# First stage of cross attention: rows of ones from another buffer, context in longer pieces, keys' weights in two parts, five values' jobs moved ahead

## The chip, the cores and the metric

The kernel runs as one program on one core of one Trainium2 chip. The metric is device time in microseconds (us) of one execution. The core has five engines that work side by side, each on its own list of instructions: PE (TensorE, matrix products), DVE (VectorE), ACT (ScalarE), POOL (GpSimd) and SP (SyncE, which here only issues DMAs). ACT issues DMAs as well. The 16 DMA engines serve both: what SP issues goes through queue q1, what ACT issues through queue q10. An engine waits for another, or for a DMA, by a semaphore (`wait_ge`).

## The reference, cut to what matters

One layer of a Perceiver: cross attention of 4 x 256 tokens on a context of 4 x 4096 rows, then attention in a window, then a mixture of 16 experts. Only the start of the first part is touched by the change.

```python
q = x @ wq.T + bq                       # x: layer norm of 4 x 256 x 256
k = y @ wk.T + bk                       # y: context, 4 x 4096 x 192
v = y @ wv.T + bv                       # 16 heads of 16
score = jnp.einsum('bhqd,bhkd->bhqk', q, k) * scale
attn = jax.nn.softmax(score, axis=-1)
out = jnp.einsum('bhqk,bhkd->bhqd', attn, v)
return out @ wo.T + bo
```

## The kernel before, in words

**Groups and steps.** Cross attention goes over 16 groups (4 batches x 4 groups of 4 heads), each of 32 steps of 128 context rows; n counts the 512 steps. Each score needs the largest score of its row first. So `max_pair(m)` computes scores with the queries as rows (2 matmuls per m, into three PSUM banks in turn) and DVE takes the largest of each (`max_one`, L1083); this runs LEAD = 36 steps ahead of the step that uses it. From n = 0 on, `scores(n)` computes the scores again with the keys as rows, ACT takes the exponential (L897), and `weigh` multiplies with the values (L537). Before n = 0 there are 36 steps with a max pair and side jobs only.

**Keys.** A job ("k", f) multiplies 2048 context rows with the keys' weights for one group (L421). ACT adds the bias into `key_low` (L884, L904), POOL splits it into a high part `key_high` and a rest `key_low` (L1447 to L1457), and SP lays both by DMA into `keys` (L1594), whose three rows 32 to 34 (and 96 to 98) of every slot must hold 1.0, so that the matmul adds the negative maximum. POOL writes 1.0 into `key_low` at the start (L1501) and SP lays it out from there into `keys` (L1617, semaphore ld_kones). Before the loop the first job is done in two halves, `keys_of(0, 0)` and `keys_of(0, 1)`, and ACT may write the first keys into `key_low` only when both DMAs that read the ones from it have landed (`e.wait_ge(ld_kones, 32)` ahead of `first_keys(0)`).

**Queries.** The first two tiles of x are normalised by DVE, turned by PE (L448), copied by ACT (L873), multiplied with `wq` (L457), taken by ACT with the bias (L878), split by POOL (L1462, L1464) and laid out by six DMAs that ACT issues (`load_q`, L396). `max_pair(0)` waits for these, for the first keys and for the ones.

**Values.** A job ("v", b, j) multiplies two tiles of context with the values' weights (L438, 6 matmuls in the program, 12 in the trace, since a float32 matmul is shown as two) and ACT empties the two PSUM banks (L910).

**The order.** It is written out by hand. `side_jobs(n)` says which side jobs stand at step n, `S_JOBS` is the list of all that use the PSUM banks S_BANKS in turn, and a job may start when ACT has emptied the one two places ahead (`bank_pair`). For batch 0 the values' jobs stand at every second step from n = -31. `turn_rows` (L466) and `q_rest` (L475) prepare the other queries.

**DMA queues.** SP issues in this order: first part of x, identf, wq, bq, rest of x, the ones (2 DMAs), the first keys, then wv, lsel, wo, bv, bo. ACT issues wk, bk and four pieces of the context (`ctx_in`).

Of the kernel before, what the change touches and what calls it, by code (L numbers as in the profile page):

```python
# [7 lines left out]
F32 = mybir.dt.float32  # L8
# [45 lines left out]
EARLY_FROM = 12  # L54
S_BANKS = (0, 2)
# [15 lines left out]
def side_jobs(n):  # L71
# [10 lines left out]
    if b < BATCH and off == 0 and 0 <= j < KT // 2:  # L82
        jobs.append(("v", b, j))
# [15 lines left out]
S_JOBS = [("k", 0)]  # L99
# [68 lines left out]
def build(nc, a, out, scratch):  # L168
    ctx = ExitStack()
    with ctx:  # L170
# [8 lines left out]
        def bank(i, n=1):  # L179
# [21 lines left out]
        ctx_in = s1.tile("ctx_in", (CB, KV // 2))  # L201
# [10 lines left out]
        wk = s1.tile("wk", (CB, EMB))  # L212
# [117 lines left out]
        ld_tok0, ld_tok1, ld_const, ld_wk, ld_wq, ld_w, ld_b, ld_c, ld_kones = semaphores(  # L330
            "ld_tok0", "ld_tok1", "ld_const", "ld_wk", "ld_wq", "ld_w", "ld_b", "ld_c", "ld_kones")
# [71 lines left out]
        def _(e):  # L403
# [5 lines left out]
            def keys_of(f, part=None):  # L409

                g, c = f // 2, f % 2 * 4
                if part is None:
                    bank_pair(("k", f))
                pairs = range(2) if part is None else (part,)
                for i in pairs:
                    e.wait_ge(ld_ctx[c // 2 + i], 16 * (g // NG + 1))
                for r in range(CB):
                    for i in pairs:
                        for odd in range(2):
                            rows, at = slice(64 * odd, 64 * odd + 64), (c // 2 + i) * CH  # L420
                            t = e.matmul(bank(S_BANKS[S_NO["k", f] % 2] + odd)[64 * i:64 * i + 64],  # L421
                                         wk[rows, r, g % NG * 64:g % NG * 64 + 64], ctx_in[rows, r, at:at + CH],
# [3 lines left out]
            def values_of(b, j):  # L426

                bank_pair(("v", b, j))
                if b == 0 and j == 0:
                    e.wait_ge(ld_w, 16 * 5)  # L430
# [3 lines left out]
                at = p * CH + j % (CH // P) * P  # L434
                for r in range(CB):
                    for odd in range(2):
                        rows = slice(64 * odd, 64 * odd + 64)
                        m = e.matmul(bank(first + odd)[:, 0:EMB], ctx_in[rows, r, at:at + P], wv[rows, r],  # L438
# [40 lines left out]
            def max_pair(m):  # L479
# [11 lines left out]
                if m == 0:  # L491
                    e.wait_ge(act_q, KE)
                    e.wait_ge(ld_kones, 32)
# [157 lines left out]
            first_queries(1)  # L651
            done_early = 0
# [217 lines left out]
        def _(e):  # L870
# [95 lines left out]
            first_queries(1)  # L966
            for n in range(-LEAD, STEPS):
# [473 lines left out]
        def _(e):  # L1441
# [59 lines left out]
            e.memset(key_low.bitcast(F32), 1.0).then_inc(pool_ones1, 1)  # L1501
# [15 lines left out]
            for n in range(-LEAD, STEPS):  # L1517
                for job in side_jobs(n):
                    if job[0] == "k":
                        split_keys(job[1])  # L1520
                    elif job == ("q", KE - 1):
# [3 lines left out]
                        e.wait_ge(ld_w, 16 * 5)  # L1525
# [59 lines left out]
        def _(e):  # L1585
# [18 lines left out]
            def load_ctx(b, p):  # L1604
                sl = slice(p * CH, (p + 1) * CH)
# [163 lines left out]
```

## Time and profile before

| | us |
|---|---|
| median of 3 runs | 1417.48 (1416.03 to 1417.87) |
| the profiled execution's own time | 1418.6 |
| its span (first to last instruction) | 1416.8 |
| PE busy | 1285.6 (91%) |
| DVE busy | 912.4 (64%) |
| ACT busy | 743.9 (53%) |
| POOL busy | 266.2 (19%) |

The whole span in 40 slices of 35.4 us, from the page (each digit is the busy share in tenths; PEld is PE loading weights, beside its matmuls):

```profile
PE   2689999999999999999999999997998729999996
PEld 1354444456444455544455544446777519999995
DVE  3478888676888767788866788627677552222224
ACT  0127777666777766677767677844555301111110
```

PE works in nine tenths and more of nearly every slice. The exceptions are the first three slices, the change from one part of the layer to the next, and the end. The change touches the first two or three slices. Times in the rows below are counted from the start of the span. A busy time is the sum of an engine's instructions; what an engine does while nobody waits for it costs nothing.

### The profile page before, as it was taken

What the parts mean: (1) busy time and instruction counts of PE and PEld (TensorE: products, weight loads), DVE (VectorE), ACT (ScalarE), POOL (GpSimd) and SP (SyncE); (2) the same over time, 40 slices, a digit from 0 to 9 for tenths busy, and PEclk for the clock granted to TensorE, in tenths of its full rate; (3) what the DMA queues carried; (4) which work ended last, traced back from release to release, by engine and by line L of the source; (5) the groups of instructions that cost most, each with busy time, mean ns of one, the idle gap of its engine ahead of it and who ended that gap; (6) DMA issues with size and microseconds to landing.
All of it is one profiled execution on the core that took longest, in us unless ns stands there. A gap on an engine that the chain in (4) does not pass through costs nothing.

```text
span 1416.8 us, 29928 instructions
## 1 busy us (share of the span) xinstructions
PE 1285.6 (91%) x12231; PEld 795.6 (56%) x12231; DVE 912.4 (64%) x1735; ACT 743.9 (53%) x1036; POOL 266.2 (19%) x245
## 2 busy tenths in 40 slices
PE   2689999999999999999999999997998729999996
PEld 1354444456444455544455544446777519999995
DVE  3478888676888767788866788627677552222224
ACT  0127777666777766677767677844555301111110
POOL 2231121211121111112112211101600012222210
PEclk7799999999999999999999999998999859999998
DMA  5735466344457334456533453100000039989852
GB/s 165 118 51 77 65 117 114 52 71 65 57 97 133 52 51 67 65 101 122 70 46 51 66 76 46 47 4 6 1 2 16 1 141 383 375 328 327 323 202 101
DMA packets 52426, 150.67 MB, mean 106 GB/s; under 512 B 17030, under 2 KB 21014, under 8 KB 44354
## 3 DMA queue, kind: packets, MB, share of 16 engines
q1 hardware_dynamic: 46562, 135.84, 43.5%
q0 software_dynamic: 2976, 8.13, 1.7%
q10 hardware_dynamic: 2752, 4.79, 1.1%
q8 instruction: 97, 1.59, 0.5%
q14 instruction: 39, 0.32, 0.1%
HBM read 88.63 MB, written 6.16 MB: 67 GB/s over the span
## 4 chain that ended last, share of the span: by engine, by line
PE 83%; DVE 7%; ACT 4%; DMA 2%; issue 2%; POOL 0%; ACTq 0%; SPq 0%; DVEq 0%; POOLq 0%
PE psum L537 19%; PE psum L519 14%; PE psum L497 10%; PE psum L829 8%; PE psum L841 8%; PE psum L438 7%; PE psum L421 6%; ACT wts L897 2%; PE psum L700 2%; DMA keys<-key_low 2%; DVE o_norm L1125 1%; PE psum L718 1%; PE psum L618 1%; DVE biased L1217 1%; DVE part_max L1083 1%
## 5 line engine op out<-in xcount | busy, mean ns | idle before, releaser
L1083 DVE TENSOR_REDUCE part_max<-psum 128x1 f32<-128x512 f32 x1024 | 656.2, 685 | 205.2 <-PE psum L497 203.8
L897 ACT ACTIVATE wts<-psum 128x1024 f32<-128x1024 f32 x512 | 515.5, 1023 | 92.1 <-PE psum L519 91.5
L537 PE MATMUL psum<-wts,vals 128*17 128x256 f32 x4096 | 317.3, 385 | 0.0
L519 PEld LDWEIGHTS psum<-queries,keys 51*128 51x128 f32 x2048 | 157.3, 185 | 201.0 <-issue 143.5
L519 PE MATMUL psum<-queries,keys 51*128 51x256 f32 x2048 | 260.2, 332 | 8.1 <-ACT wts L897 7.0
L497 PE MATMUL psum<-keys,queries 51*128 51x512 f32 x1024 | 229.4, 443 | 24.9 <-DVE part_max L1083 11.1
L1029 ACT ACTIVATE hid<-psum,b1s 128x128 f32<-128x128 f32 x124 | 35.4, 367 | 206.7 <-PE psum L829 170.0
L537 PEld LDWEIGHTS psum<-wts,vals 128*17 128x17 f32 x4096 | 69.5, 95 | 120.7 <-issue 97.2
L497 PEld LDWEIGHTS psum<-keys,queries 51*128 51x128 f32 x1024 | 97.2, 185 | 40.1 <-DVE part_max L1083 26.4
L829 PE MATMUL psum<-xTt,w1s 128*128 128x128 f32 x992 | 118.0, 278 | 0.0
L829 PEld LDWEIGHTS psum<-xTt,w1s 128*128 128x128 f32 x992 | 115.4, 195 | 0.3 <-issue 0.2
L841 PE MATMUL psum<-w2s,hid 128*128 128x256 f32 x496 | 112.0, 379 | 0.0
L1447 POOL CAST key_high<-key_low 128x1024 fp32r<-128x1024 f32 x31 | 32.1, 1037 | 407.0 <-ACT key_low L904 402.8
L421 PE MATMUL psum<-ctx_in,wk 64*64 64x512 f32 x768 | 97.8, 620 | 9.9 <-DMA ctx_in<-in_ctxT 9.9
L438 PE MATMUL psum<-wv,ctx_in 64*128 64x256 f32 x768 | 99.5, 392 | 0.0
L841 PEld LDWEIGHTS psum<-w2s,hid 128*128 128x128 f32 x496 | 91.9, 190 | 11.3
L1407 DVE TENSOR_SCALAR hid<-psum,b1s 128x128 f32<-128x128 f32 x124 | 34.9, 344 | 95.9 <-PE psum L829 95.9
L438 PEld LDWEIGHTS psum<-wv,ctx_in 64*128 64x128 f32 x768 | 70.9, 188 | 27.7 <-issue 16.4
L983 ACT ACTIVATE wt<-biased,nmax 128x160 f32<-128x160 f32 x128 | 44.3, 416 | 76.4 <-DVE nmax L1219 76.4
L910 ACT ACTIVATE vals<-psum 128x512 f32<-128x512 f32 x64 | 38.3, 598 | 86.2 <-PE psum L438 86.2
L904 ACT ACTIVATE key_low<-psum,bk 128x1024 f32<-128x1024 f32 x31 | 34.5, 1113 | 89.2 <-PE psum L421 89.2
L1449 POOL TENSOR_TENSOR key_low<-key_low,key_high 128x1024 fp32r<-128x1024 f32 x31 | 73.6, 2374 | 2.5
(180 smaller groups left out, 985.0 us busy)
## 6 DMA issues: line engine op xcount, KB each, us to landing
keys<-key_high SPq DMA_DIRECT2D x256, 128.0 KB, 4.5
w1s<-in_W SPq DMA_DIRECT2D x31, 1024.0 KB
w2s<-in_W SPq DMA_DIRECT2D x31, 1024.0 KB
keys<-key_low SPq DMA_DIRECT2D x128, 128.0 KB, 6.4
ctx_in<-in_ctxT SPq DMA_DIRECT2D x12, 768.0 KB, 9.2
ctx_in<-in_ctxT ACTq DMA_DIRECT2D x4, 768.0 KB, 22.4
queries<-query_high SPq DMA_DIRECT2D x60, 32.0 KB, 5.4
rows_x<-xn SPq DMA_DIRECT2D x2, 512.0 KB, 2.7
```

What stands on the lines that cost most here:

```text
L421: t = e.matmul(bank(S_BANKS[S_NO["k", f] % 2] + odd)[64 * i:64 * i + 64], wk[rows, r, g % NG * 64:g % NG * 64 + 64], ctx_in[rows, r, at:at ...
L438: m = e.matmul(bank(first + odd)[:, 0:EMB], ctx_in[rows, r, at:at + P], wv[rows, r], start=(r == 0), stop=(r == CB - 1))
L497: e.matmul(bank(M_BANKS[(2 * m + i) % 3]), queries[g % 3][64 * i:64 * i + STK, hh, qt * P:(qt + 1) * P], keys[64 * i:64 * i + STK, hh, slo ...
L519: m = e.matmul(bank(S_BANKS[S_NO["s", n] % 2] + i)[:, hh * SEQ:(hh + 1) * SEQ], keys[64 * i:64 * i + STK, hh, c, at:at + P], queries[g % 3 ...
L537: i = e.matmul(bank(O_BANK)[32 * j:32 * j + VW, 0:SEQ], vals[:, t, h * VW:(h + 1) * VW], wts[n % NW][:, j * SEQ:(j + 1) * SEQ], start=(t = ...
L829: i = e.matmul(bank(2 * (j % 2) + hb)[:, q * P:(q + 1) * P], w1s[j % RING][:, k, hc * P:(hc + 1) * P], xTt[j % 2][:, k], start=(k == 0), s ...
L841: i = e.matmul(bank(4 + j % 2)[:, 0:EMB], hid[j % 2][:, hc], w2s[j % RING][:, hc], start=(hc == 0), stop=(hc == HC - 1))
L897: i = e.activation(wts[n % NW], s_bank(job, 2), ACT.Exp, scale=QSCALE)
L910: i = e.activation(vals[:, t:last + 1:CH // P].rearrange("p t (h w) -> p t h w", w=VW)[:, :, :, 0:HD], s_bank(job, 2).rearrange("p (t h w) ...
L983: i = e.activation(wt2[r][:, j], biased[r][:, j], ACT.Exp, bias=nmax[r][:, j:j + 1])
L1083: e.reduce_max(part_max[g % 2][:, hq, c:c + 1], bank(M_BANKS[n % 3]), AX_X).then_inc(dve_max, 1)
L1449: e.tensor_tensor(key_low, key_f, key_high.bitcast(F32), ALU.subtract).then_inc(pool_low, 1)
```

## The change

Five edits, all ahead of the steady part:

1. The 1.0 that is laid out into `keys` is now written into `wo` (27 of its 128 partitions are read) and goes in four DMAs of 27 pieces of 4 KB instead of two of 54. These stand on SP's queue right behind x and identf, ahead of wq and bq. ACT does not wait for ld_kones any more before it writes the first keys; SP waits for it before it loads lsel and wo; `max_pair(0)` waits for it as before.
2. The context is laid out in memory so that each partition gets one piece of 6 KB per DMA instead of three of 2 KB.
3. The keys' weights come in two parts: those of group 0 first (768 bytes per partition), the rest behind the second context piece. The rest of x moves from SP's queue to ACT's, between the second and the third context piece.
4. wv has its own semaphore and stands on SP's queue ahead of the first keys.
5. The values' jobs j = 0 to 4 of batch 0 are done before `max_pair(0)`, not at n = -31 to -23. ACT has a small exponential of identf at the start, and its table load (L884 before) goes with it.

```diff
-S_JOBS = [("k", 0)]
+S_JOBS = [("k", 0)] + [("v", 0, _j) for _j in range(FIRST_V)]      # FIRST_V = 5
-        ctx_in = s1.tile("ctx_in", (CB, KV // 2))
+        ctx_in = s1.tile("ctx_in", (NCH // 2, CB * CH))
...  PE
                 if m == 0:
                     e.wait_ge(act_q, KE)
-                    e.wait_ge(ld_kones, 32)
+                    e.wait_ge(ld_kones, 64)
...
             first_queries(1)
+            for j in range(FIRST_V):
+                values_of(0, j)
...  ACT
-            for dst, src in ((wk, "wkT"), (bk, "bk")):
-                e.dma_start(dst, a[src]).then_inc(ld_wk, 16)
+            e.dma_start(wk[:, 0], a["wkT"][:, 0]).then_inc(ld_wk, 16)
+            e.dma_start(bk, a["bk"]).then_inc(ld_wk, 16)
             for p in range(NCH // 2):
-                sl = slice(p * CH, (p + 1) * CH)
-                e.dma_start(ctx_in[:, :, sl], a["ctxT"][0, :, :, sl]).then_inc(ld_ctx[p], 16)
+                e.dma_start(ctx_in[:, p], a["ctxT"][0, p]).then_inc(ld_ctx[p], 16)
+                if p == 1:
+                    e.dma_start(wk[:, 1:], a["wkT"][:, 1:]).then_inc(ld_wk, 16)
+                    e.dma_start(x[:, BT:], a["x"][:, BT:]).then_inc(ld_tok1, 16)
+            e.wait_ge(ld_const, 16)
+            e.activation(inverse[:, 0:P], identf, ACT.Exp)
             e.wait_ge(ld_wk, 32)
-            e.wait_ge(ld_kones, 32)
             first_keys(0)
...
             first_queries(1)
+            for j in range(FIRST_V):
+                empty(("v", 0, j))
...  POOL
-            e.memset(key_low.bitcast(F32), 1.0).then_inc(pool_ones1, 1)
+            e.memset(wo, 1.0).then_inc(pool_ones1, 1)
...  SP
             e.dma_start(identf, a["identf"]).then_inc(ld_const, 16)
+            e.wait_ge(pool_ones1, 1)
+            for at in (NEG, 64 + NEG):
+                for hh in range(2):
+                    e.dma_start(keys[at:at + NP, hh].rearrange("r s k -> r (s k)").bitcast(F32),
+                                wo[0:NP * SLOTS // 2].rearrange("p a b -> p (a b)")).then_inc(ld_kones, 16)
             e.dma_start(wq, a["wqT"]).then_inc(ld_wq, 16)
             e.dma_start(bq, a["bq"]).then_inc(ld_wq, 16)
-            e.dma_start(x[:, BT:], a["x"][:, BT:]).then_inc(ld_tok1, 16)
-            e.wait_ge(pool_ones1, 1)
-            for at in (NEG, 64 + NEG):
-                e.dma_start(keys[at:at + NP].rearrange("r h s k -> r (h s k)").bitcast(F32),
-                            key_low[0:NP * SLOTS].bitcast(F32)).then_inc(ld_kones, 16)
+            e.dma_start(wv, a["wvT"]).then_inc(ld_wv, 16)
             for part in range(2):
                 e.wait_ge((pool_firsth, pool_firstl)[part], 1)
                 scatter_pair(0, 0, part, ld_first)
-            for dst, src in ((wv, "wvT"), (lsel, "lsel"), (wo, "woT"), (bv, "bv"), (bo_bc, "bo")):
+            e.wait_ge(ld_kones, 64)
+            for dst, src in ((lsel, "lsel"), (wo, "woT"), (bv, "bv"), (bo_bc, "bo")):
```

The DMAs that SP issues from the start of the program, in order, before the change (out<-in and shape; `keys<-key_low 3x18x1024` are the ones, L1594 the first keys):

```order
L1610 DMA x<-in_x 128x512
L1611 DMA identf<-in_identf 128x128
L1612 DMA wq<-in_wqT 128x512
L1613 DMA bq<-in_bq 128x2
L1614 DMA x<-in_x 128x1536
L1617 DMA keys<-key_low 3x18x1024 x2
L1594 DMA keys<-key_high 16x2x1024 x4
```

and after it, at the same place of SP's list:

```order
L1619 DMA x<-in_x 128x512
L1620 DMA identf<-in_identf 128x128
L1624 DMA keys<-wo 3x9x1024 x4
L1626 DMA wq<-in_wqT 128x512
L1627 DMA bq<-in_bq 128x2
L1628 DMA wv<-in_wvT 128x768
L1604 DMA keys<-key_high 16x2x1024 x4
```

The ones have moved from behind wq, bq and the rest of x to ahead of wq; wv has come ahead of the first keys; the rest of x has gone from this queue.

PE's matmuls from the first ones on, before (L421 keys, L448 turned rows, L457 first queries, L497 max pairs, L438 values, L466 turned rows of the rest):

```order
L421 MATMUL psum<-ctx_in,wk 64x512 x6
L448 MATMUL psum<-identf,xn_91 128x128 x4
L457 MATMUL psum<-xT_92,wq 128x256 x2
L421 MATMUL psum<-ctx_in,wk 64x512 x6
L457 MATMUL psum<-xT_92,wq 128x256 x2
L497 MATMUL psum<-keys,queries_69 128x512 x2
L421 MATMUL psum<-ctx_in,wk 64x512 x12
L497 MATMUL psum<-keys,queries_69 128x512 x10
L438 MATMUL psum<-wv,ctx_in 128x256 x6
L497 MATMUL psum<-keys,queries_69 128x512 x2
L466 MATMUL psum<-identf,xn_91 128x128 x6
```

and after (the same jobs, at L424, L451, L460, L500, L441, L469 and, for the rest of the queries, L478), from the second half of the first keys on:

```order
L424 MATMUL psum<-ctx_in,wk 64x512 x6
L460 MATMUL psum<-xT_92,wq 128x256 x2
L441 MATMUL psum<-wv,ctx_in 128x256 x30
L500 MATMUL psum<-keys,queries_69 128x512 x2
L424 MATMUL psum<-ctx_in,wk 64x512 x12
L500 MATMUL psum<-keys,queries_69 128x512 x12
L469 MATMUL psum<-identf,xn_91 128x128 x6
L500 MATMUL psum<-keys,queries_69 128x512 x8
L469 MATMUL psum<-identf,xn_91 128x128 x6
L500 MATMUL psum<-keys,queries_69 128x512 x8
L478 MATMUL psum<-xT_92,wq 128x384 x4
```

Five values' jobs (30 matmuls) stand ahead of the first max pair, and none between it and the first job of L478 (`q_rest`), where five stood.

## Rows read from the trace of the kernel before

**Rows 1.** Page, part 4: shares of the chain that ended last, by engine.

```profile
PE 83%; DVE 7%; ACT 4%; DMA 2%; issue 2%; POOL 0%; ACTq 0%; SPq 0%; DVEq 0%; POOLq 0%
```

**Rows 2.** Chain in order of time, 0 to 110: start us, us, what.

```profile
2.60 0.47 SPq L1614
...
4.11 23.70 DMA keys<-key_low
...
27.86 1.28 ACT L884
29.16 1.12 ACT key_low L884
...
35.15 0.67 ACTq L396
...
38.41 6.68 DMA queries<-query_high
...
62.33 1.30 PE psum L438 x12
```

**Rows 3.** Waits in 0 to 80: who waited for whom, us, times, longest.

```profile
ACT L884 <- DMA keys<-key_low: 27.9, 1, 27.9
```

**Rows 4.** Timeline, 0 to 80: start us, us, engine, line, instruction, count, idle before.

```profile
0.73 0.95 POOL L1501 MEMSET key_low<- 128x1024 f32 x1 [0.29 <-POOLq L1757]
...
9.90 4.75 PE L421 MATMUL psum<-ctx_in,wk 64*64 64x512 f32 x12 [9.90 <-DMA ctx_in<-in_ctxT]
...
30.89 2.04 PE L457 MATMUL psum<-xT,wq 128*128 128x256 f32 x4 [15.65 <-ACT xT L873]
...
45.18 0.79 PE L497 MATMUL psum<-keys,queries 51*128 51x512 f32 x2 [7.73 <-DMA queries<-query_high]
45.90 5.40 PE L421 MATMUL psum<-ctx_in,wk 64*64 64x512 f32 x24
...
53.87 0.49 PE L497 MATMUL psum<-keys,queries 51*128 51x512 f32 x2 [0.78 <-DVE part_max L1083]
55.15 0.79 PE L497 MATMUL psum<-keys,queries 51*128 51x512 f32 x2 [0.78 <-DVE part_max L1083]
56.72 0.80 PE L497 MATMUL psum<-keys,queries 51*128 51x512 f32 x2 [0.78 <-DVE part_max L1083]
59.51 0.99 PE L497 MATMUL psum<-keys,queries 51*128 51x512 f32 x2
61.82 0.50 PE L497 MATMUL psum<-keys,queries 51*128 51x512 f32 x2
...
72.22 2.85 PE L475 MATMUL psum<-xT,wq 128*128 128x384 f32 x8
...
75.00 0.50 PE L497 MATMUL psum<-keys,queries 51*128 51x512 f32 x2
```

**Rows 5.** DMA issues, 0 to 80: out<-in, KB each, median us from issue to landing.

```profile
x<-in_x SPq DMA_DIRECT2D x1, 768.0 KB, 8.3
...
queries<-query_high SPq DMA_DIRECT2D x4, 32.0 KB, 4.0
```

**Rows 6.** DMA queues in 18 to 24: packets, MB, share of 16 engines' time.

```profile
q10 hardware_dynamic: 48, 0.09, 10.4%
q1 hardware_dynamic: 47, 0.18, 8.7%
```

**Rows 7.** Windows: us, busy by engine, PE's granted clock, DMA share, GB/s.

```profile
1.00:2.00 1.00, 0.00 (x0) 0.00 (x0) 0.40 (x1) 0.00 (x0) 0.94 (x2) 1.00 0.21 29
...
10.00:16.00 6.00, 5.24 (x16) 1.65 (x16) 4.59 (x25) 0.00 (x0) 0.00 (x0) 1.00 1.04 327
16.00:28.00 12.00, 0.00 (x0) 0.00 (x0) 2.35 (x8) 0.14 (x1) 0.00 (x0) 0.55 0.20 49
...
51.00:55.00 4.00, 1.81 (x10) 0.64 (x6) 3.15 (x5) 1.11 (x1) 2.38 (x2) 0.93 0.07 15
55.00:61.00 6.00, 5.07 (x21) 3.39 (x22) 3.73 (x7) 0.60 (x1) 1.02 (x1) 0.50 1.03 143
```

More of the change, by code:

```diff
@@ L54 @@
 EARLY_FROM = 12
+FIRST_V = 5
 S_BANKS = (0, 2)
@@ L81, in side_jobs @@
     j, off = divmod(at - (1 if b == 0 else 7), 2 if b == 0 else 3)
-    if b < BATCH and off == 0 and 0 <= j < KT // 2:
+    if b < BATCH and off == 0 and (FIRST_V if b == 0 else 0) <= j < KT // 2:
         jobs.append(("v", b, j))
@@ L211, in build @@
         query_low = s1.tile("query_low", (KE, TOK), F32R)
-        wk = s1.tile("wk", (CB, EMB))
+        wk = s1.tile("wk", (NG, CB * 64))
         wv = s1.tile("wv", (CB, EMB))
@@ L413, in keys_of @@
                     bank_pair(("k", f))
+                if f == 2:
+                    e.wait_ge(ld_wk, 48)
                 pairs = range(2) if part is None else (part,)
@@ L419, in keys_of @@
                         for odd in range(2):
-                            rows, at = slice(64 * odd, 64 * odd + 64), (c // 2 + i) * CH
+                            rows = slice(64 * odd, 64 * odd + 64)
                             t = e.matmul(bank(S_BANKS[S_NO["k", f] % 2] + odd)[64 * i:64 * i + 64],
-                                         wk[rows, r, g % NG * 64:g % NG * 64 + 64], ctx_in[rows, r, at:at + CH],
+                                         wk[rows, g % NG, r * 64:(r + 1) * 64], ctx_in[rows, c // 2 + i, r * CH:(r + 1) * CH],
                                          start=(r == 0), stop=(r == CB - 1))
@@ L429, in values_of @@
                 if b == 0 and j == 0:
-                    e.wait_ge(ld_w, 16 * 5)
+                    e.wait_ge(ld_wv, 16)
                 p = j // (CH // P)
@@ L433, in values_of @@
                 first = S_BANKS[S_NO["v", b, j] % 2]
-                at = p * CH + j % (CH // P) * P
                 for r in range(CB):
+                    at = r * CH + j % (CH // P) * P
                     for odd in range(2):
                         rows = slice(64 * odd, 64 * odd + 64)
-                        m = e.matmul(bank(first + odd)[:, 0:EMB], ctx_in[rows, r, at:at + P], wv[rows, r],
+                        m = e.matmul(bank(first + odd)[:, 0:EMB], ctx_in[rows, p, at:at + P], wv[rows, r],
                                      start=(r == 0), stop=(r == CB - 1))
@@ L1524, in _ @@
                         e.memset(ones_in[:, KT - TT:], 1.0).then_inc(pool_vones, 1)
-                        e.wait_ge(ld_w, 16 * 5)
+                        e.wait_ge(ld_w, 16 * 4)
                         e.wait_ge(dve_rows1, TT)
```

13 lines of the change are left out of this document (6 added, 7 removed).

## The prediction

> **What bounds the kernel now.** I read the page first (the chain of waits and the 40 slices), then the waits, the timeline, the DMAs and the windows of the first 80 us, where the change lies. PE makes 83% of the chain that ended last, DMA 2% [rows 1]; so over the whole program a saving counts only if it lets PE's list run sooner. In the first 45 us it is another picture [rows 2]. The longest piece of the chain is not work but one DMA: the rows of ones, issued last at 4.1 and followed for 23.70 us. ACT stands idle for 27.9 us until they have landed [rows 3], because the ones are read from the tile that it has to write. Then follow the table load (1.28), the first keys (1.12), the queries and their six DMAs, the last issued at 38.41 and landed 6.68 later [rows 2]. PE had done its first keys (9.90, 4.75 long), idled 15.65 us ahead of the first queries at 30.89, and started max pair 0 only at 45.18 [rows 4]. From there on PE and DVE are kept busy by the written order, and no row there shows a wait for a load. So I ask two things: how much sooner max pair 0 starts, and whether the steps behind it take as long as before. What they gain together should reach the end undiminished: steps, groups and the later stages start from one another.
>
> **The ones, and what stands behind them.** They are 432 KB before and after, 108 pieces of 4 KB. How fast do they go? The rest of x ahead of them in the same queue was issued at 2.60 [rows 2] and landed 8.3 us later [rows 5], at 10.9, and the ones end at 27.8: some 17 us, where 432 KB at the 327 GB/s of 10 to 16 would take 1.3 [rows 7]. In 16 to 28 the DMA share is 0.20, three of 16 engines, at 49 GB/s for both queues [rows 7]. Three rows go to three engines: 36 pieces on each, and per engine one piece every 17 / 36 = 0.47 us. In 18 to 24 those engines took 47 packets from q1 and 48 from q10 [rows 6]: one for one.
>
> The page "DMA: Bandwidth & Descriptors" of the Trainium skill (section on why a DMA increments its semaphore by 16) says that a DMA uses the largest number of engines up to 16 that divides both slowest dimensions, and the lowest numbered. That is 3 for 3 rows from 54 and 3 for 3 rows from 27. The share of 0.20 agrees. By that rule the four DMAs bring nothing over the two: again 36 pieces on each of the same engines, and wq queues behind them.
>
> I take three engines again, since both shapes have three rows, and 17 us. The start: POOL's fill ends at 1.68 [rows 4], SP issues at 1.7, and the first DMA of all, issued at 0.73, has the engines moving within 1 to 2 (share 0.21, [rows 7]), about 1.1 later. So the ones start at 2.9 and land at 19.9 instead of 27.8. The context pieces get longer: q10 now gives 6 KB for each of its turns. An engine moves 327 / 16 = 20.4 GB/s, so a turn of each queue is 10 KB or 0.49 us, about the 0.47 measured; bounds are 0.47 (the ones are limited by their common target) and 0.47 plus 4 KB more of q10 at 20.4 (0.20), 0.67, which makes 24.1 us.
>
> wq, which before had landed long before use, now stands behind the ones. On the three engines it is 8 packets of 2 KB, each beside 6 KB of context: 8 x 8 KB / 20.4 = 3.2 us. So the weights of the queries land at W = 2.9 + 17 + 3.2 = **23.1** (30.2 by the slow bound). The first context piece has 48 KB per engine, 8 turns, and its issue time is unchanged; PE's first keys start at 9.9 or up to 3 earlier, which is cover either way: with 4.75 of keys, 1.12 and the copy they end long before 23.1. The table load (1.28, [rows 2]) goes under the same cover: worth nothing beyond the end of the 27.9 us wait. The rest of x, later in q10, and the other weights of the keys are needed after 40; at nothing. If W came early they would still be in by then.
>
> **From W to max pair 0.** PE's first queries start at W. Before, from there (30.89) to the first issue of a queries' DMA (35.15) it took 4.3 [rows 2, 4], and to the last issue (38.41) 7.5; ACT is free 0.6 later. Its own path: W + 8.2 = 31.3, first_keys(1) 1.12 [rows 2], 32.4. Here the moved values come in. The first has both banks free, the second needs that ACT has emptied the second half of the keys, so values 2 to 5 start at 32.4 and follow at 1.30 each [rows 2] (half clock: twice that) with small waits for ACT, 1.33: 5.3 us. Max pair 0 can start at **37.7**. The other condition, the queries' last DMA, is issued at W + 7.5 = 30.6 and lands after 4.0 (SP's, with less traffic, [rows 5]) to 6.7 (before): 34.6 to 37.3. So the values replace the DMA as last condition, by 0.4 to 3 us. Gain at this point 45.18 - 37.7 = **7.5 us**.
>
> **The steps behind it.** Before, from max pair 0 to the one behind the first q_rest: 45.18 to 75.00, 29.8 us. The five values are out of it, and their cost there is smaller than their 1.3 to 2.8 us each, since DVE sets the pace beside them. Without side jobs one pair follows another after 1.28 us (53.87 to 55.15) at full clock and after 1.57 (55.15 to 56.72) at half, 1.2 GHz [rows 4]. Which clock? In 51 to 55 PE was busy for 1.81 of 4.00 us, with max pairs only, and in 55 to 61 the granted clock was 0.50, though PE was then busy for 5.07 of 6 [rows 7]. After the change PE has just such pairs for 13 steps, with two turn_rows. So I count: pair 0 and keys 1 at full clock, as PE comes out of 14 us of nearly unbroken work, half of 5.40 + 0.6 = 3.3 (before 6.05, half clock); then 13 intervals to the pair ahead of q_rest: 4 at 1.28, 7 at 1.57 and 2 with turn_rows at half clock at 2.31 (59.51 to 61.82) = 20.7; then that pair 0.8 and q_rest, 2.85 at full clock, begun at half, 4.6. Sum 29.4 against 29.8, gain **0.4 us**. At full clock throughout it would be 3.3 + 11 x 1.28 + 2 x 1.4 + 3.3 = 23.5, gain 6.3; with half clock from the first pair, 6.0 + 11 x 1.57 + 4.6 + 6.5 = 34.4, loss 4.6.
>
> **Elsewhere.** lsel and wo now wait for the ones at 19.9; before they were issued at 36, so this costs nothing. The 12 later context loads were not waited for before, and 6 KB pieces change nothing there: 0, bounds -0.5 to 0.5.
>
> **Sum.** 7.5 + 0.4 = 7.9 us. Of the profiled execution's own 1418.6 (its span of 1416.8 and 1.8 around it) that leaves 1410.7. That execution stands 1.1 above the median of the runs shown, 1417.48; against the median the forecast is **1409.6 us**.
>
> **Rivals.**
> A. The forecast. Chance 0.50; range 1406 to 1412.5.
> B. The clock stays at 2.4 GHz over the pairs: 5.9 us more, **1403.7**. For it: PE comes to max pair 0 after long work, and has weight loads beside the matmuls. Against it: the drop in [rows 7] came behind the same pairs. Chance 0.20.
> C. The four DMAs take other engines than the first three, or wq does not queue behind them: W at about 15, where ACT has copied the turned rows. Then max pair 0 could start at W + 14.6 = 29.6: gain 15.6 and 0.4, **1401.5**. Only the smaller pieces speak for it. Chance 0.08.
> D. The ones go at the slow bound: W = 30.2, max pair 0 at 44.8, gain 0.4 and 0.4: **1416.7**; halfway, 1413. For it: at the beginning all 16 engines are loaded. Chance 0.15, a third of it within 0.2% of no change.
> E. Slower than before. The ones and the longer context pieces share badly. On the three engines q10 moved 2 KB in each turn of 0.47; if that is their rate for context beside ones, 6 KB cost 3 x 0.47 = 1.41 us a turn, 36 turns 51 us, as far as q10 has work: its 48 packets do. W about 55, max pair 0 near 70, **1442**. It decides from W = 31 on, that is 0.70 us a turn. Against it: q10 had no more than 2 KB to give in a turn, and 20.4 GB/s elsewhere. A milder form with half clock in all steps (loss 4.6) and W past 26.4 gives 1418 to 1422. Together 0.07.
>
> The page "DMA: Bandwidth & Descriptors" (section on queues, rings and completion order) says that an engine takes turns between the queue rows packet by packet; 47 to 48 [rows 6] agrees. By this rule longer packets let the context load more in each turn and leave the number of turns of the ones at 36, as A has it.
>
> **How the numbers follow.** Faster by over 0.2% (2.8 us; about what can be told from no change) is below 1414.7: all of A, B, C and two thirds of D, 0.50 + 0.20 + 0.08 + 0.09, rounded to 0.86. Within 0.2%: 0.07; slower 0.07. The range of 8 in 10 leaves out most of C and the worse part of D and E: 1401.8 to 1414.6.
>
> **What would show it.** Right: ACT's first keys at 12 to 15 with no wait for the ones; PE idle from about 14 until 23 ahead of the first queries, ended by the load of wq; ones landed near 20; max pair 0 at about 38 with a value's matmul right ahead of it; pairs 1.57 apart and a clock of 0.50 between 44 and 60; the pair behind q_rest at about 67; from there on the steps as before. Wrong: first queries at 15 (C), or after 30 (D, E); pairs 1.28 apart up to q_rest (B); max pair 0 waiting for the queries' DMAs; or a new wait for context or for values further on, which would eat the gain.

## The result, and the profile after

| | before | after |
|---|---|---|
| median of 16 runs each, same chip | 1418.08 (1415.61 to 1420.63) | 1420.59 (1418.34 to 1423.92) |
| the profiled execution's span | 1416.8 | 1419.7 |

The ratio is 1.0016, 95% interval [1.0009, 1.0024]: the kernel became 0.16% slower, where 0.6% faster was forecast. The time lies 6 us above the range.

The chain of waits of after, in order of time (start us, us, what), is the counterpart of [rows 2]:

```profile
5.48 27.18 DMA bq<-in_bq
...
32.70 2.09 PE psum L460 x4
...
36.72 0.68 ACTq L397
...
40.65 1.12 ACT key_low L889
...
41.81 5.45 PE psum L441 x48
47.26 0.24 PE psum L500 x2
...
71.75 4.21 PE psum L478 x8
```

The ones' DMA (23.70 us in [rows 2]) is gone from the chain, and the bias of the queries, a DMA of 1 KB, stands there with 27.18 us. It is not slow itself: it stands on SP's queue behind wq, and wq behind the ones. The waits of the first 80 us (who waited for whom, us, times, longest) say who pays now, against ACT's 27.9 us in [rows 3]:

```profile
ACT qf L883 <- PE psum L460: 19.1, 1, 19.1
...
PE psum L460 <- DMA bq<-in_bq: 18.1, 1, 18.1
...
ACT key_low L909 <- DMA keys<-key_low: 3.4, 1, 3.4
```

The last of these rows is ACT's wait ahead of the keys of job 1; PE did not wait for those keys.

And the timeline, for the same places as [rows 4] (start us, us, engine, line, instruction, count, idle before and what ended it):

```profile
1.70 3.17 SPq L1624 DMA_DIRECT2D keys<-wo  x4
...
9.42 4.63 PE L424 MATMUL psum<-ctx_in,wk 64*64 64x512 f32 x12 [9.42 <-DMA wk<-in_wkT]
...
28.95 0.33 SPq L1634 DMA_DIRECT2D lsel<-in_lsel  x1
...
32.70 2.08 PE L460 MATMUL psum<-xT,wq 128*128 128x256 f32 x4 [18.07 <-DMA bq<-in_bq]
...
41.81 5.45 PE L441 MATMUL psum<-wv,ctx_in 64*128 64x256 f32 x48 [0.60 <-ACT key_low L889]
...
46.91 0.59 PE L500 MATMUL psum<-keys,queries 51*128 51x512 f32 x2
...
54.00 0.70 PE L500 MATMUL psum<-keys,queries 51*128 51x512 f32 x2 [0.78 <-DVE part_max L1093]
55.48 0.80 PE L500 MATMUL psum<-keys,queries 51*128 51x512 f32 x2 [0.78 <-DVE part_max L1093]
57.05 0.80 PE L500 MATMUL psum<-keys,queries 51*128 51x512 f32 x2 [0.78 <-DVE part_max L1093]
...
71.68 4.28 PE L478 MATMUL psum<-xT,wq 128*128 128x384 f32 x8
75.89 0.50 PE L500 MATMUL psum<-keys,queries 51*128 51x512 f32 x2
```

SP issues lsel once the ones have landed: at 28.95. That row dates them in every kernel below in which SP stands idle for them (not in e9, e10, e12 and e13, where SP was busy with keys until then). Max pair 0 stands at 46.91 (before 45.18), with a value's matmuls right ahead of it, and the pair behind the first `q_rest` at 75.89 (before 75.00).

The windows of after (us, busy by engine, PE's granted clock, DMA share, GB/s), beside [rows 7]:

```profile
5.00:9.00 4.00, 0.00 (x0) 0.00 (x0) 3.10 (x17) 1.59 (x2) 0.53 (x2) 1.00 0.96 315
9.00:16.00 7.00, 5.22 (x16) 1.81 (x16) 0.00 (x0) 1.59 (x2) 0.61 (x1) 1.00 1.02 349
16.00:23.00 7.00, 0.00 (x0) 0.00 (x0) 0.00 (x0) 0.00 (x0) 2.75 (x2) 0.54 0.85 172
23.00:27.00 4.00, 0.00 (x0) 0.00 (x0) 1.55 (x5) 0.00 (x0) 0.00 (x0) 0.50 0.19 65
...
54.00:75.00 21.00, 14.70 (x40) 7.35 (x41) 14.71 (x23) 1.62 (x2) 1.97 (x1) 0.51 0.56 75
115.00:123.00 8.00, 7.46 (x58) 3.01 (x54) 5.17 (x9) 3.40 (x4) 0.00 (x0) 0.57 0.89 109
```

The first four are the time of the ones: until 16 all engines are loaded, until 23 the first keys go beside them, and only then are they left with what remains of the context on three engines (0.19 = 3 of 16). The pairs run at half clock, 1.2 GHz, from 54 on, as forecast. The last row was not forecast: the clock falls once more near n = 0, where the trace of before has full clock (1.00 in 115 to 123), and the steps there take 2.75 us longer (start times of the same max pairs in both traces: 0.88 us late at pair 36, 3.63 late at pair 52; 2.9 us at the end of the span).

### The profile page after: what moved, and what is told of

Its sections match the earlier page's. It is cut to its first block, busy times and chain, and to the rows that moved or that the text cites. A ratio compares the mean times of both kernels' runs of the same rounds, so it can differ in the third digit from the quotient of the medians.

```text
span 1419.7 us, 29933 instructions
## 1 busy us (share of the span) xinstructions
PE 1287.9 (91%) x12231; PEld 795.8 (56%) x12231; DVE 912.6 (64%) x1735; ACT 744.1 (52%) x1037; POOL 266.2 (19%) x245
## 3 DMA queue, kind: packets, MB, share of 16 engines
q1 hardware_dynamic: 43352, 135.05, 42.8%
## 4 chain that ended last, share of the span: by engine, by line
PE 83%; DVE 8%; ACT 3%; issue 2%; DMA 2%; ACTq 0%; SPq 0%; POOL 0%; DVEq 0%; POOLq 0%
PE psum L540 19%; PE psum L522 14%; PE psum L500 10%; PE psum L834 8%; PE psum L846 8%; PE psum L441 6%; PE psum L424 6%; ACT wts L902 2%; DMA bq<-in_bq 2%; PE psum L705 2%; DVE o_norm L1135 2%; DVE part_max L1093 1%; PE psum L621 1%; DVE biased L1227 1%; PE psum L723 1%
## 5 line engine op out<-in xcount | busy, mean ns | idle before, releaser
L500 PE MATMUL psum<-keys,queries 51*128 51x512 f32 x1024 | 231.1, 447 | 21.1 <-DVE part_max L1093 15.1
L500 PEld LDWEIGHTS psum<-keys,queries 51*128 51x128 f32 x1024 | 98.1, 186 | 37.8 <-DVE part_max L1093 31.9
L424 PE MATMUL psum<-ctx_in,wk 64*64 64x512 f32 x768 | 95.6, 606 | 9.4 <-DMA wk<-in_wkT 9.4
L441 PE MATMUL psum<-wv,ctx_in 64*128 64x256 f32 x768 | 97.9, 389 | 0.6 <-ACT key_low L889 0.6
L441 PEld LDWEIGHTS psum<-wv,ctx_in 64*128 64x128 f32 x768 | 69.9, 186 | 28.5 <-issue 16.8
L993 ACT ACTIVATE wt<-biased,nmax 128x160 f32<-128x160 f32 x128 | 44.3, 416 | 76.9 <-DVE nmax L1229 76.9
```

The lines of the kernel that those rows point to most:

```text
L441: m = e.matmul(bank(first + odd)[:, 0:EMB], ctx_in[rows, p, at:at + P], wv[rows, r], start=(r == 0), stop=(r == CB - 1))
L500: e.matmul(bank(M_BANKS[(2 * m + i) % 3]), queries[g % 3][64 * i:64 * i + STK, hh, qt * P:(qt + 1) * P], keys[64 * i:64 * i + STK, hh, slo ...
L993: i = e.activation(wt2[r][:, j], biased[r][:, j], ACT.Exp, bias=nmax[r][:, j:j + 1])
```

## The experiments

All times are medians; the ratio is to the kernel before, run beside it. "Pair 0" is the start of max pair 0 in the trace, "V" the number of values' jobs ahead of it. There is one trace per kernel. after and e3 are the same up to the first queries, and yet their ones landed at 28.95 and 28.15 and their first queries started at 32.70 and 30.84; the stretch from the last max pair to the end, which no kernel here changes, took 519.3 to 522.0. So a difference between two traces is not read below 1 to 2 us.

| kernel | V | us (runs) | ratio, 95% interval | pair 0 |
|---|---|---|---|---|
| after | 5 | 1420.59 (16) | 1.0016 [1.0009, 1.0024] | 46.9 |
| e1 weights ahead of ones | 5 | 1412.49 (6) | 0.9961 [0.9948, 0.9974] | 35.6 |
| e2 context in 2 KB pieces | 5 | 1420.77 (11) | 1.0015 [1.0006, 1.0024] | 44.2 |
| e3 no values ahead | 0 | 1413.23 (6) | 0.9967 [0.9955, 0.9979] | 40.6 |
| e4 before, ACT released only | 0 | 1413.94 (6) | 0.9974 [0.9961, 0.9987] | 41.4 |
| e5 ones by row | 5 | 1418.70 (11) | 1.0003 [0.9994, 1.0012] | 44.3 |
| e6 e1, ones in two parts | 5 | 1407.88 (5) | 0.9929 [0.9915, 0.9942] | 33.1 |
| e7 the same | 0 | 1408.20 (5) | 0.9925 [0.9911, 0.9938] | 27.4 |
| e8 as e1 | 0 | 1408.11 (5) | 0.9935 [0.9921, 0.9948] | 35.4 |
| e9 second part sooner | 0 | 1407.24 (5) | 0.9928 [0.9914, 0.9941] | 33.4 |
| e10 the same | 5 | 1409.03 (5) | 0.9944 [0.9930, 0.9957] | 33.1 |
| e11 keys wait again | 5 | 1417.59 (10) | 1.0005 [0.9996, 1.0015] | 42.8 |
| e12 second part behind keys | 0 | 1401.89 (4) | 0.9891 [0.9874, 0.9907] | 27.8 |
| e13 the same | 5 | 1406.54 (5) | 0.9920 [0.9907, 0.9934] | 30.8 |
| e16 e8, ones on two queues | 0 | 1411.06 (5) | 0.9951 [0.9937, 0.9964] | 38.6 |

e14 and e15 measure the ones alone and have one run each, 1419.91 and 1419.79.

### What stands behind the ones (e1, e3, e4)

e1 is the kernel after with wq, bq and wv issued ahead of the ones:

```diff
+            e.dma_start(wq, a["wqT"]).then_inc(ld_wq, 16)
+            e.dma_start(bq, a["bq"]).then_inc(ld_wq, 16)
+            e.dma_start(wv, a["wvT"]).then_inc(ld_wv, 16)
             e.wait_ge(pool_ones1, 1)
...  the ones
-            e.dma_start(wq, a["wqT"]).then_inc(ld_wq, 16)
-            e.dma_start(bq, a["bq"]).then_inc(ld_wq, 16)
-            e.dma_start(wv, a["wvT"]).then_inc(ld_wv, 16)
```

> The changed kernel with one thing put back: wq and bq (and wv) are issued on SP's queue ahead of the ones. Queue theory (the queries' weights wait behind the ones on three DMA engines, and that wait of 18 us ahead of the first queries is what ate the gain): the first queries start at about 15 instead of 32.7, max pair 0 waits for the ones and the first keys behind them instead, at 31 to 34 (46.9 in the changed kernel); about 13 us faster than the changed kernel, 1405 to 1409. Values theory (the five values' jobs ahead of max pair 0 are the cost): max pair 0 stays above 44, the time within 2 us of 1420.6. Context theory (6 KB pieces slow every queue): wq lands early but the ones land at 29 or later, and the gain stays under 8 us.

8.1 us sooner than after: the place of wq behind the ones is a main part of the fault. It is 3.5 us above the range of 1405 to 1409, and that has its row in e1's timeline, where the first keys are now the transfer that is stuck behind the ones:

```profile
33.44 0.34 SPq L1634 DMA_DIRECT2D lsel<-in_lsel  x1
...
35.56 0.51 PE L500 MATMUL psum<-keys,queries 51*128 51x512 f32 x2 [2.20 <-DMA keys<-key_low]
```

e3 sets FIRST_V = 0 in the kernel after: no values ahead.

> The changed kernel with no values' job moved ahead (FIRST_V = 0). Queue theory: the first queries still start at 32.7; max pair 0 no longer waits for values but for the queries' last DMA, at 42 to 43 instead of 46.9; the steps up to the pair behind the first q_rest take 0.5 to 2 us more than 29.0; 2.5 to 4 us faster than the changed kernel, 1417 to 1418. Values theory (they are the main loss): 5 us or more faster, 1415.5 or less. If the moved values were worth their place: no faster, 1420 or more.

The first queries (W) started at 30.8, pair 0 came at 40.6 instead of 46.9, and the kernel is 7.4 us faster than after. So the five values cost more than the change lost in all. From pair 0 to the pair behind the first `q_rest` e3 takes 27.5 us with the five jobs among the pairs, after 29.0 without them: the steps did not get shorter, and their clock was lower (0.50 for some 7 of the 27.5 us in e3, for 20 of the 29.0 in after). e4 is the kernel before with only ACT's wait taken away, by reading the ones from another buffer:

```diff
-            e.wait_ge(ld_kones, 32)                                  # ACT, ahead of the first keys
-            e.memset(key_low.bitcast(F32), 1.0)
+            e.memset(wo, 1.0)
-                            key_low[0:NP * SLOTS].bitcast(F32)).then_inc(ld_kones, 16)
+                            wo[0:NP * SLOTS].rearrange("p a b -> p (a b)")).then_inc(ld_kones, 16)
+            e.wait_ge(ld_kones, 32)                                  # SP, ahead of wv
```

> The kernel before with one edit: the ones are read from wo, ACT does not wait for them any more, SP waits for them before wv and wo. Everything else, the place of the ones on the queue too, is as before. Queue theory: wq is there at 6, first keys at about 15, the queries are laid out by 27, max pair 0 waits for the ones (27.8) and the first keys behind them: 29 to 32 instead of 45.2, 13 to 16 us faster than before, 1402 to 1406. Values theory and context theory say nothing against that; if something else of the start is the limit (another load behind the ones), max pair 0 comes after 36.

The wait of 27.9 us was gone and gave 4.3 us, not 13 to 16. e4's chain names what came late instead, the queries' DMAs, which ACT issued while the ones and the context were on the three engines (against 6.68 us in [rows 2]):

```profile
26.63 14.71 DMA queries<-query_high
```

The ones account for the first 3 us of these 14.71 only: they had landed when SP issued wv at 29.70. The rest of the time SP's wv, lsel, wo and keys went through the same engines (DMA share 0.83 in 30 to 34 and 1.08 in 34 to 37). Which of them held the queries up no run separates.

### How fast the ones go (e2, e5, e11, e14, e15)

e2 lays the context in pieces of 2 KB again (`ctx_in` as (CB, KV // 2)), with all else of after.

> The changed kernel with the context in three pieces of 2 KB per partition and DMA, as before. Context theory (each of the 36 turns of the ones is longer, about 0.64 us, because q10 gives 6 KB in its turn): turns of 0.47 us, the ones land near 23 instead of 28.9, the first queries start near 26.5 instead of 32.7, max pair 0 near 41, time about 1414.5. If the length of the pieces has nothing to do with it: the ones at 28 to 30 and 1420 to 1421.5.

The ones landed at 26.6 instead of 28.9 (e3: 28.15) and W was 30.0, between the two branches; pair 0 came at 44.2, and the time is that of after. The long pieces cost the ones 1.5 to 2.3 us and are not the main cause of the loss. e2's trace is 2.7 us ahead of that of after at the last max pair and 0.6 at the end; the difference arises in stages that the change does not touch. e5 lays the ones out in six DMAs of one row each, for nine engines (in the trace each raises its semaphore ten times, where each of those on three engines does so four times):

```diff
-                for hh in range(2):
-                    e.dma_start(keys[at:at + NP, hh]...
+                for r in range(at, at + NP):
+                    e.dma_start(keys[r:r + 1]...
```

> The changed kernel with the ones laid out by six DMAs of one row each (18 pieces of 4 KB from 18 partitions) instead of four of three rows; nothing else. Engine theory (the ones are slow because three DMA engines carry 36 pieces each): with nine engines each carries 12 pieces, the ones land before 15 instead of 28.9, wq with them, the first queries start near 16 instead of 32.7, max pair 0 at 30 to 33 instead of 46.9, and the time is 1405 to 1410. Target theory (writes to the three neighbouring rows share one way in, about 26 GB/s, whichever engine brings them): the ones land at 23 to 28 as in the changed kernel, the first queries start at 27 to 32, and since more engines are held up behind them the time is 1417 to 1422.

They landed at 23.6, 18.3 us after their first packet at 5.3: 432 KB at 24 GB/s on nine engines. With 17.6 us on three in the kernel before (10.2 to 27.8), three times the engines bring nothing. The first queries still waited until 29.88, 6.3 us longer: in 16 to 20 all the engines were busy (share 1.00) and moved 106 GB/s. Why the engines without ones were held up too is not shown. e11 puts ACT's wait for the ones back into after, so that no keys go beside them.

> The changed kernel with ACT's wait for the ones put back ahead of the first keys, so that the first keys' six DMAs do not run beside the ones. Target theory (these DMAs write into the same groups of rows and took 3 to 4 us from the ones): the ones land at 24.5 to 26 instead of 28.9 and wq 3 us sooner, the first queries start near 29 to 30 instead of 32.7; max pair 0 at 43 to 45, the time 1417 to 1420. If the first keys' DMAs do not slow the ones: landed at 28 to 29 as in the changed kernel, and the time is above 1420.6, since the keys come later too.

ACT's wait ended at about 26.5, 21.4 us after the first packet at 5.1, against 23.4 in after and 22.6 in e3: the DMAs of the first keys had cost the ones 1 to 2 us. e14 holds the context as well, until the ones have landed:

```diff
+            e.wait_ge(ld_kones, 64)                                  # ACT, ahead of its context loads
             for p in range(NCH // 2):
```

> The kernel after, with ACT's loads of the context held until the ones have landed: a measurement of the ones alone, not a faster kernel. Theory (the ones are limited by the rows that they are written to; the load beside them, context and the first keys, costs the rest of the 23.4 us): first packet at about 3 to 4, all landed within 14 to 17.5 us of it, so the first context load is issued at 18 to 21; at least 25 GB/s, no more than 32. Rival (their three engines are the limit, at the 20.4 GB/s that an engine moves with long pieces): 432 KB over three engines take 7 us, context issued at 10 to 11. Max pair 0 is late in this kernel by as much as the context is, so its time, some 1418 to 1424, says nothing.

The context was issued at 19.98, so the ones took 16.7 us alone from their first packet at 3.3, by the same measure as the 23.4 of after; their last packet ended at 19.1, which is 15.8 us and 28 GB/s. In 11 to 17 hardly anything else moved (packets; queue: packets, MB, share of 16 engines):

```profile
DMA packets 45, 0.17 MB, mean 29 GB/s; under 512 B 3, under 2 KB 3, under 8 KB 45
...
q1 hardware_dynamic: 45, 0.17, 19.4%
```

29 GB/s with three engines busy all the time: 10 GB/s each, where each moved 20.4 in [rows 7]. So it is not the engines that set the pace, and what is left is the rows that are written or those that are read. The time of e14, 1419.91 in one run, tells nothing of the change. e15 sends the two groups of rows side by side, 32 to 34 through SP's queue and 96 to 98 through ACT's:

> The kernel of e14 (no context load until the ones have landed) with the ones of rows 96 to 98 on ACT's queue and those of rows 32 to 34 on SP's, side by side instead of one behind the other. Theory (each group of rows has a limit of its own of about 29 GB/s): the 15 us of e14 become 7.5 to 9, and ACT issues the context at 11.5 to 13.5 instead of 20.0. Rival 1 (one limit for all these rows): 14 to 17.5 us, context at 18 to 21. Rival 2 (the three engines that both groups share limit them, at the 20.4 GB/s that an engine moves in long pieces): 7.2 us, hard to tell from the theory here; the length of one 4 KB piece tells it: 0.2 us by the engine's rate, about 0.45 if it waits for its rows. Its time says nothing on the kernel.

The context was issued at 15.51, 12.1 us after the first packet at 3.4: between the theory and its first rival. Two groups at once are faster than one, so there is not one limit for all six rows, and the rows that are read, the same for both groups, are not the limit of 28 GB/s either: what fits e5, e14 and e15 is a limit of each group that is written. A limit of each queue on each engine would fit e14 and e15, but not e5, where nine engines bring no more than three. But the 7.5 us of two full limits was not reached, while the same three engines also had wq and wv to load. The length of a piece, which was to tell the theory from rival 2, was 0.28 us on average against 0.43 in e14, between the 0.2 and the 0.45 that were expected, so it does not decide. How much is which stays open.

The page "SBUF — State Buffer" of the Trainium skill (section "Door 1: The DMA port swizzle") says that DMAs reach the partitions through 16 ports of eight partitions each, where 32 to 35 share a port with 0 to 3, and 96 to 99 one with 64 to 67. "DMA: Bandwidth & Descriptors" (section "Where 436 GB/s comes from") gives 435 GB/s for the 16 ports. An estimate by these: 27.2 GB/s for a group, 16.3 us for both in turn, and longer by the share of context and keys that goes through the same ports. The 28 to 29 GB/s of e14 agree within 7%, e5 agrees, and e15 only in part. The prediction had looked at the rule on engines, not at this one.

### Ones in two parts (e6, e7, e9, e10, e12, e13), and on two queues (e16)

Pairs 0 to 15 read only four slots of `keys`. e6 is e1 with 96 KB of ones first and 336 KB behind the queries' DMAs of SP; `max_pair(16)` waits for them. e7 is the same with V = 0, and e8 is e1 with V = 0. SP's wait for the ones and its loads of lsel, wo, bv and bo have moved too: behind the second part and ahead of the keys of job 1 in e6 and e7, behind those keys in e9, e10, e12 and e13. How much of the gain over e1 and e8 is theirs no run shows.

```diff
+                if m == 16:
+                    e.wait_ge(ld_kones2, 128)
...  SP, instead of the ones in one go
+                    e.dma_start(keys[at:at + NP, hh, SLOT_OFF:SLOT_OFF + 4]...
...  and behind load_q(e, 1)
+            for lo, hi in ((SLOT_OFF + 4, SLOTS), (0, SLOT_OFF)):
+                        e.dma_start(keys[at:at + NP, hh, lo:hi]...then_inc(ld_kones2, 16)
```

> The changed kernel with wq, bq and wv ahead of the ones and the ones in two parts: 96 KB for the four slots that the first keys go to at the old place, the other 336 KB behind the queries of group 1 on SP's queue, waited for at max pair 16. Queue theory: 24 pieces are 8 turns on each of the three engines, landed near 14; the first keys are not held up; max pair 0 is bound by PE's and ACT's own work and the five values, 29 to 32; 15 us faster than the changed kernel, 1404 to 1408. Values theory: no better than the kernel with weights first by more than 1 us (1412.5).

> As the ones in two parts, with no values' job moved ahead. If the moved values only delay max pair 0: max pair 0 at 25 to 28, 3 to 5 us faster than with five of them, 1400 to 1404. If the steps after it are then longer by the same amount: equal to it within 1.5 us.

e6's time came as expected, with pair 0 at 33.1, 1 us later than that. e7 had pair 0 earliest of all and lost it again at pair 16. Its keys came late because SP, which issues them, stood waiting for the second part ahead of lsel (7.3 us, until 48.57) and issued them only from 50.38 on:

```profile
63.96 0.80 PE L502 MATMUL psum<-keys,queries 51*128 51x512 f32 x2 [7.15 <-DMA keys<-key_low]
```

```profile
SPq L1644 <- DMA keys<-wo: 7.3, 1, 7.3
```

> The kernel with weights first (1412.5 measured, max pair 0 at 35.6, bound by the landing of the first keys behind the ones) with no values' job moved ahead. The values are hidden under that wait, so max pair 0 stays at 34 to 36; what changes is the stretch behind it, where the jobs come back between the pairs: PE's clock stays up, and the time is within 1.5 us of 1412.5. If the values delayed it after all: 1408 or less.

This fell: e8 is 4.4 us faster than e1 with pair 0 at the same place, so where pair 0 waits anyway, values ahead of it are not harmless. The traces show where 2.3 us of it arise: 0.9 up to the pair behind `q_rest`, 1.4 in a fall of the clock near n = 0 that e1 has and e8 has not. The rest is not found in the steps. The next two move the second part ahead, right behind the first keys.

> As the ones in two parts without values moved, with the second part of the ones issued right behind the first keys (at 21 instead of 35), and the wait for it with lsel, wo, bv, bo behind the keys of job 1. Target theory (336 KB at 24 to 26 GB/s are 13 to 14 us whenever they go): landed at 35 to 38, so keys 1 are laid out from 42 on and the pair 16 does not wait, which it did by 8 us; max pair 0 stays at 28 to 30; 6 us faster than 1408.2, 1400 to 1403. If the rest of the ones holds up the queries and the second half of the first keys: max pair 0 or pair 8 comes 5 us or more later and the time is 1406 or more.

> The same with five values' jobs ahead of max pair 0. From the runs so far (7.4 us between the changed kernel and the one without moved values, 4.4 with weights first): max pair 0 is 4 to 6 us later than without them, the steps behind give back 0 to 2, the time is 3 to 6 us above the kernel without moved values. If their place is as good: equal within 1.5 us.

Pair 16 did not wait any more, but in e9 the queries' last DMA took 9.37 us beside the ones and put pair 0 at 33.4, the branch "1406 or more". e10 was 1.8 us slower than e9, below the 3 to 6 expected: pair 0 waited in e9 for as long as the values took. e12 differs from e9 in one thing: the second part stands behind the keys of the other half.

> The kernel of e9 with the second part of the ones (336 KB, eight DMAs) issued behind the DMAs of the first pair's keys and ahead of those of the queries; the wait for them, and the load of lsel behind it, behind the keys of job 1; no values moved ahead. Theory (the ones take some 13 to 15 us wherever they stand, and cost time only where something needed soon stands behind them on the queue or on their three engines): max pair 0 at 28 to 29 as in e7, the second part issued at about 31.5 to 37.5 and landed at 44 to 46, pair 16 waits under 2 us instead of the 7.2 of e7, and the time is 1398 to 1402. Rival (the keys of job 1 stand behind the ones on those engines): the wait of pair 16 stays at 3 us or more and the time is 1404 or more.

1401.89 us, 16.3 below before in its span: the fastest of all. Two rows of its timeline show why: pair 0 waits only for the queries, and pair 16 for 0.7 us of keys. The second part landed by 47.9, later than expected, and nothing needed it sooner.

```profile
27.77 0.80 PE L502 MATMUL psum<-keys,queries 51*128 51x512 f32 x2 [6.55 <-DMA queries<-query_high]
...
57.76 0.50 PE L502 MATMUL psum<-keys,queries 51*128 51x512 f32 x2 [0.68 <-DMA keys<-key_low]
```

> The kernel of e12 with the five values ahead of max pair 0 again. Theory (they start when the second half of the first keys is copied, and put max pair 0 later by about 5 us, of which their absence from the steps gives back 2 to 3): max pair 0 at 31 to 33 against 27.7, the time 1.5 to 4 us above e12, 1403.5 to 1406. Rival (they fill time in which PE would wait for the queries' DMAs): within 1 us of e12. On the clock: if the fall near 100 us depends on where PE's list stands in time, it may come at another place or not at all, which is up to 2.8 us either way.

The five values cost 4.65 us, more than the 1.5 to 4 expected. Two windows show where: with the values ahead (e13, first) a stretch of 26 us that begins some us behind pair 0 runs at a clock of 0.54, without (e12, second) at 0.91. Half the clock makes the pairs, which DVE paces, 1.57 apart instead of 1.28, and the work between them twice as long. In the two traces the pair behind `q_rest` comes 5.75 us later with the values; at the end 2.5 are left, mostly because e12's trace has a fall of the clock near n = 0 that costs 2.9, and e13's has none.

```profile
36.00:62.00 26.00, 18.34 (x52) 9.05 (x54) 16.89 (x27) 2.48 (x3) 3.38 (x2) 0.54 0.67 106
```

```profile
30.00:56.00 26.00, 21.32 (x134) 12.93 (x128) 18.16 (x29) 6.33 (x9) 4.84 (x4) 0.91 0.79 117
```

Last, e16: the kernel e8 with the ones of rows 96 to 98 on ACT's queue, behind context and x.

> The kernel of e8 (weights of queries and values ahead of the ones, no values moved ahead) with the ones of rows 96 to 98 on ACT's queue behind its loads of context and x, those of rows 32 to 34 on SP's as in e8. Theory: the ones of SP's queue, half as many, are in 8 to 11 us sooner than the 33.4 of e8, so the first keys behind them are too; max pair 0 at 27.5 to 30 instead of 35.4, the rest as in e8: 1400.5 to 1403. Rival (all share one limit, or the queries' DMAs, which are behind the ones on ACT's queue now, become the last): max pair 0 at 33 or later, 1406 or more.

A miss, by the rival's way. The queries' DMAs now stood behind ones on ACT's queue: pair 0 at 38.6 after a wait of 17.1 us for them, 1411.06 us.

## Why the prediction was wrong, step by step

What failed is the first term, the time of the ones, and with it W. The parts behind it, down to the pair behind `q_rest`, were sized right; the fall of the clock near n = 0 was not in the sum.

| step | forecast | measured | by |
|---|---|---|---|
| first packet of the ones | 2.9 | 5.5 | trace of after |
| the ones take | 17 | 23.4 | first packet to lsel at 28.95 |
| wq and bq behind them | 3.2 | 3.7 | first queries at 32.70 |
| W | 23.1 | 32.7 | |
| W to max pair 0 | 14.6 | 14.2 | 46.91 |
| max pair 0 to the pair behind q_rest | 29.4 | 29.0 | 75.89 |
| gain there | 7.9 | -0.9 | |
| further falls of the clock | 0 | 2.75 | window 115 to 123 |

**The ones.** "I take three engines again ... and 17 us" had the engines right and the 17 us taken from a quieter time. In before the ones began at 10.2, by their first packet, and ran mostly beside a trickle, 49 GB/s for both queues in 16 to 28 [rows 7]. In after they ran from 5.5 while all queues moved 315 to 349 GB/s, then beside the first keys. e14 gives them 16.7 us with next to nothing else. Of the 6.7 us on top of that, e11 gives about 2 to the keys and e2 about 1 to the long pieces (26.6 less a first packet at 4.4 is 22.2), where after and e3, the same up to there, differ by 0.8. The rest goes with the remaining load; no run splits it further. The bound of 0.67 us a turn for 36 turns, 24.1 us, which the prediction had worked out and given 0.15 (rival D), comes near the 23.4, but by luck: it is made of the longer pieces alone, and e2, without them, still has 22.2. With the later start W came to 32.7, past the 31 from which rival E decides, though not by E's price. The prediction did name a limit at the "common target", but took 0.47 us a turn as its full price under any load. Its other bound asked what the engines could carry, and e5, e14 and e15 show that the limit is not there.

**The start.** The ones were issued from 1.7 on and moved at 5.5, not at 2.9. The kernel with context in 2 KB pieces (e2) has 4.4, the one without context (e14) 3.3. So some 1.1 us belong to the length of the pieces ahead and 1.1 to the context as such, each from one trace. The last 0.4 us stay open.

**The values.** Priced right where they stand (forecast 5.3 us, measured 5.4). What the prediction had wrong is what they replace: it let the queries' last DMA take 4.0 to 6.7 us, so that the values would cost 0.4 to 3. In after that DMA took 2.0 us and ACT's last copy of the queries ended at 42.3, so the values alone held pair 0 for 4.7 us more. Nor do the steps get shorter without the values: from pair 0 to the pair behind `q_rest` they take 28.9 to 30.3 us in the ten traces with V = 5 and 27.5 to 30.0 in the eight with V = 0. Three pairs of kernels that differ in V alone give the net price: 7.4 us (after, e3), 4.4 (e1, e8), 4.65 (e13, e12), each give or take 2 to 3 by the intervals of the table, and 1.8 and about 0, neither clear of noise, where pair 0 or pair 16 waits for a DMA (e10, e9; e6, e7).

**Clock.** Rival B (full clock over the pairs) fell: 0.51 in 54 to 75. Rival C (W at 15) fell: wq did queue behind the ones.

**Where the expected gain went.** ACT's wait for the ones, 27.9 us, was replaced by PE's wait of 18.1 us for wq and bq behind the same ones. The first queries start 1.8 us later than before (32.70 against 30.89), max pair 0 1.7 later; the steps behind it, without the values, give 0.8 back, the clock near n = 0 takes 2.75, and 0.7 comes back by the end: 2.9. e12 shows that the gain was there, 1.1%, when nothing that is needed soon stands behind the ones and no values stand ahead of pair 0.

## What to carry to other kernels

A transfer into a few rows is slow wherever it starts, and moving it ahead moves its slowness ahead of everything on its queue and on its engines: list what stands behind it and when that is needed, and put it behind the last urgent one, in parts if some of it is needed soon. Keep the engine that issues the transfers from waiting for the slow one ahead of an urgent issue (e7). Take the duration of such a transfer from a stretch as loaded as the one it moves into. Work that is pulled out of steps paced by another engine left those steps as long as they were here, and added its length in front.

## What the runs showed of the hardware that was not expected

- Six rows in two groups took 432 KB in 16.7 us alone, 17.6 us under a light load and 23.4 us under a heavy one on three engines, and 18.3 us on nine (e5); both groups at once took 12.1 us.
- A DMA of 32 KB can take many times its own time: those of the queries took 2.0 us in after, when little else was under way, 9.37 in e9 beside the ones, 6.68 in before beside the weights and keys of SP, and 14.71 in e4 beside the end of the ones and then these weights and keys.
- The granted clock falls to 0.50 once more near n = 0, for 3 to 7 us, in the profiles of after, e1, e2, e5, e6, e10, e11, e14 and e15, all with five values ahead, and of e12, with none; not in before, e3, e4, e7, e8, e9 and e16, with none, nor in e13, with five. From pair 36 to pair 52 it takes 23.6 us without the fall, 25.0 with the short one and 26.2 to 26.4 with the long one. In e12 it stands thus, and costs 2.9 us:

```profile
96.00:104.00 8.00, 7.83 (x60) 3.07 (x60) 4.81 (x9) 3.18 (x4) 0.00 (x0) 0.57 0.78 101
```

  The instructions there are the same in all of them. Nine of the ten profiles with five values ahead have the fall, and one of the eight without. So the values go with it but do not decide it: e12 and e13 each break the rule. With one profile per kernel it is not known whether the fall comes in every execution of a kernel. The cause is open.
